# Graph attention on one core: start-up work moved between engines, and the context of blocks 1 to 3 divided by ScalarE in operations of one head

## What is computed

```python
h  = maximum(layernorm(x), 0)                   # sources
hs = layer_norm(h, ln1)                         # masked by nodemask
ht = layer_norm(h_target, ln1)
q = (ht @ Wq + bq) / sqrt(32);  k = hs @ Wk + bk;  v = hs @ Wv + bv
logits = where(adj != 0, q k^T, -1e30)          # [8, 2048, 2048]
ctx = softmax(logits) @ v                       # [2048, 256]
ht = layer_norm(ht + ctx @ Wo + bo, ln2)
out = x + ht + gelu(ht @ W1) @ W2
```

## Time and profile before

| | us |
|---|---|
| median of 3 runs | 715.5 |
| lowest, highest | 714.21, 716.79 |
| the profiled execution, its own time | 714.83 |
| its span, first to last instruction | 713.0 |
| PE busy | 665.8 (93%) |
| DVE busy | 584.3 (82%) |
| POOL busy | 535.8 (75%) |
| ACT busy | 457.4 (64%) |
| mean granted TensorE clock | 0.986 of full |

### The profile page before, as it was taken

The page is one execution under the profiler, slowest core; times in us unless marked ns, Lnnn a source line. Parts: engine busy times, 40 slices in busy tenths (PEclk is TensorE's granted clock), DMA queues, the critical chain, the costliest instruction groups (busy, mean ns, idle before and its releaser), DMA issues. The chain is left out here.

```text
span 713.0 us, 20226 instructions
## 1 busy us (share of the span) xinstructions
PE 665.8 (93%) x8326; PEld 474.8 (67%) x8326; DVE 584.3 (82%) x961; ACT 457.4 (64%) x816; POOL 535.8 (75%) x508
## 2 busy tenths in 40 slices
PE   4987979999999999999999999999999899989998
PEld 4545657676776667667766776777667567657667
DVE  5987768989999977999999699988986988674651
ACT  4644547676776646787766586777655787767550
POOL 3647849889999966799999678999976787552430
PEclk9998989999999999999999999999999999999999
DMA  8721630203000010130010111103000000000001
GB/s 292 263 57 38 208 108 3 90 32 109 28 3 32 2 60 31 61 105 2 2 32 2 60 61 55 38 2 121 2 1 2 2 2 2 2 1 31 16 23 51
DMA packets 20795, 36.20 MB, mean 51 GB/s; under 512 B 2752, under 2 KB 13280, under 8 KB 20704
## 3 DMA queue, kind: packets, MB, share of 16 engines
q1 hardware_dynamic: 20704, 34.92, 15.8%
HBM read 26.49 MB, written 2.10 MB: 40 GB/s over the span
## 5 line engine op out<-in xcount | busy, mean ns | idle before, releaser
L1351 POOL TENSOR_TENSOR prob_lo<-prob 128x512 f16<-128x512 f32 x382 | 436.2, 1166 | 80.8 <-ACT prob L859 80.1
L859 ACT ACTIVATE prob<-score 128x512 f32<-128x512 f32 x512 | 305.1, 597 | 173.4 <-PE score L451 166.2
L451 PE MATMUL early<-kT,qT 96*128 96x512 f16 x512 | 193.9, 384 | 18.7 <-DVE half_max L1140 17.9
L451 PE MATMUL score<-nidentb,mask_nat 128*128 128x128 bf16 x2048 | 200.0, 221 | 3.6 <-ACT qT L876 1.9
L451 PEld LDWEIGHTS ctx<-v_sb,prob 128*128 128x128 bf16 x2048 | 159.8, 98 | 59.8 <-ACT raw L881 10.4
L451 PE MATMUL score<-qT,kT 97*128 97x512 f16 x512 | 197.1, 385 | 0.0
L451 PE MATMUL ctx<-v_sb,prob 128*128 128x65 f16 x2048 | 192.6, 193 | 2.5 <-POOL prob_lo L1351 1.7
L1140 DVE CUSTOM_DVE_ANT_0 early<-early,mask_nat,half_max 128x1024 f32<-128x1024 f32 x128 | 163.0, 1285 | 34.6 <-PE early L451 33.1
L451 PE MATMUL ctx<-v_sb,prob_lo 128*128 128x65 f16 x2048 | 191.4, 193 | 0.0
L1140 DVE CUSTOM_DVE_ANT_0 early<-early,mask_nat 128x1024 f32<-128x1024 f32 x128 | 156.8, 1228 | 25.7 <-PE early L451 24.3
L451 PEld LDWEIGHTS ctx<-v_sb,prob_lo 128*128 128x128 f16 x2048 | 143.7, 97 | 50.3 <-issue 5.1
(11 more groups left out here) (164 smaller groups left out, 615.5 us busy)
## 6 DMA issues: line engine op xcount, KB each, us to landing
adj_in<-in_adj SPq DMA_DIRECT2D x26, 512.0 KB, 3.8
qT<-q_stage SPq DMA_DIRECT2D x48, 64.0 KB, 2.0
kT<-mask_nat SPq DMA_DIRECT2D x48, 64.0 KB, 2.0
raw<-in_x SPq DMA_DIRECT2D x4, 512.0 KB, 5.4
tgt<-in_L_gnn_h_target SPq DMA_DIRECT2D x4, 512.0 KB, 11.8
prob<-in_adj SPq DMA_DIRECT2D x4, 512.0 KB, 10.3
nT<-in_L_gnn_W SPq DMA_DIRECT2D x2, 1024.0 KB, 7.3
mask_nat<-in_x SPq DMA_DIRECT2D x1, 2048.0 KB, 8.5
```

The source lines that it names most:

```text
L451: return nc.tensor.matmul(dst, w, m, start=start, stop=stop, **more)
L859: nc.scalar.activation(prob[:, n % SLOTS, :], score[n % 2][:, :], ACT.Exp).then_inc(exp_done, 1)
L1351: nc.gpsimd.tensor_tensor(prob_lo[:, n % SLOTS, :], prob[:, n % SLOTS, :], prob_hi(n % SLOTS), ALU.subtract).then_inc(lo_sem["pool"], 1)
```

## The change

Ten edits, in five groups.

1. **Start-up, masks of block 0.** Tiles 4 to 7 are made by POOL (`make_mask` in the POOL program, after its memsets) and not by DVE, and counted on a semaphore of their own, `mask_pool`. DVE makes tiles 0 and 1 ahead of `low_parts(3)` and 2 and 3 behind it.
2. **Start-up, feature sum.** POOL's six folds and DVE's reduction go. ACT makes the sum of each half of the features in one operation of 128x2048 with an accumulating output, one ahead of `high_parts(4)` and one behind it.
3. **Start-up, order on PE and SP.** The value products 3 to 7 follow the early products 1 to 5 one by one. SP issues the first two adjacency loads of block 1, then the third and fourth group of placements, and only then waits for the values and loads W1 and W2.
4. **Tables.** The first mask of a next block is made in unit 1 at j = 0 (was unit 0, j = 6), the second at (2, 3) (was (2, 4)). `CT_AT` goes from (2, 6), (2, 11) to (2, 3), (2, 7); the first `WO_AT` from (2, 13) to (2, 11). The last context sum goes from (2, 1) to (1, 11).
5. **The division.** For blocks 0 to 2 (made during blocks 1 to 3) ACT divides, two heads a step: two operations of 128x32 with the reciprocal as a per-partition scale, in four steps for each of the four tiles, beginning at (0, 7), (1, 1), (1, 7) and (1, 12). DVE keeps the division of block 3 and the reciprocals.

```diff
-CT_AT = {(2, 6): 0, (2, 11): 1}
-WO_AT = {(2, 13): 0, (3, 1): 1}
+CT_AT = {(2, 3): 0, (2, 7): 1}
+WO_AT = {(2, 11): 0, (3, 1): 1}
-MASK_DVE = [(0, 6), (2, 4), (2, 6), (3, 2), (3, 7), (4, 3), (4, 7), (5, 3)]
-LOAD_AT = [0, 0, 0, 2, 2, 3, 4, 4]
+MASK_DVE = [(1, 0), (2, 3), (2, 6), (3, 2), (3, 7), (4, 3), (4, 7), (5, 3)]
+LOAD_AT = [0, 0, 1, 2, 2, 3, 4, 4]
-SUM_AT = [(0, 3), (0, 11), (1, 5), (2, 1)]
-NORM_AT = [(0, 5), (1, 1), (1, 5), (2, 2)]
+SUM_AT = [(0, 3), (0, 11), (1, 5), (1, 11)]
+NORM_AT = [(0, 7), (1, 1), (1, 7), (1, 12)]
+NORM_STEPS = H // 2
...
 # SP
                 for c in (2, 3):
                     place_k(c, range(1, 2))
-
-                sp.wait_ge(v_ready, NT // 2)
-                sp.wait_ge(feat_done, 1)
-                for i, (dst, w) in enumerate(((w1, W1), (w2, W2))):
-                    sp.dma_start(dst, w.rearrange("(c p) n -> p c n", p=P)).then_inc(w_in[i], 16)
+                for i in range(2):
+                    load_adj(1, i)
                 for g in range(2, TT):
                     place_q(0, range(g, g + 1))
                     for c in range(NTB):
                         place_k(c, range(g, g + 1))
+                sp.wait_ge(v_ready, NT // 2)
+                sp.wait_ge(feat_done, DC)
+                for i, (dst, w) in enumerate(((w1, W1), (w2, W2))):
+                    sp.dma_start(dst, w.rearrange("(c p) n -> p c n", p=P)).then_inc(w_in[i], 16)
...
 # PE
                 project(4)
-                for e in range(1, TT):
+                for e in range(1, RAMP + 2):
                     for i in range(2):
                         early_scores(e, i)
-                    values(e + 2)
-                values(6)
-                values(7)
-                for e in range(TT, RAMP + 2):
-                    for i in range(2):
-                        early_scores(e, i)
+                    if e + 2 < NT // 2:
+                        values(e + 2)
...
 # ACT
+                def feature_sum(c):
+                    act.wait_ge(nT_masked, DC * NTB)
+                    nc.scalar.activation(unread[:, c, :, :], nT[:, :, c, :], ACT.Copy, accum_out=feat_all[:, c:c + 1]).then_inc(feat_done, 1)
+                def context_norm(k, t, part):
+                    if t == 0 and part == 0:
+                        act.wait_ge(den_done, k + 1)
+                        for g in range(TT):
+                            act.wait_ge(q_placed[g], PLACE * (k + 2))
+                    if part == 0:
+                        act.wait_ge(csum_done, TT * k + t + 1)
+                    for h in (2 * part, 2 * part + 1):
+                        last = nc.scalar.activation(cnorm[:, t, h * HD:(h + 1) * HD], raw_of(k)[:, t, h, 0:HD], ACT.Copy,
+                                                    scale=rden[:, t * H + h:t * H + h + 1])
+                    if part == NORM_STEPS - 1:
+                        last.then_inc(cn_done, 1)
...
                 high_values(2)
+                feature_sum(0)
                 high_parts(4)
+                feature_sum(1)
...
 # ACT, each step, behind the exponential and the other jobs of the step
                         if k > 0:
+                            for part in range(NORM_STEPS):
+                                if (r, s - part) in NORM_AT:
+                                    context_norm(k - 1, NORM_AT.index((r, s - part)), part)
...
 # DVE
-                for i in range(TT):
+                for i in range(2):
                     make_mask(0, i)
                 low_parts(3)
+                for i in range(2, TT):
+                    make_mask(0, i)
+                maxima(0)
                 low_values(2)
-                maxima(0)
-                make_mask(0, 4)
+                maxima(1)
                 low_parts(4)
-                for e in range(1, TT):
+                for e in range(2, RAMP + 1):
                     maxima(e)
-                    make_mask(0, e + 4)
-                for e in range(TT, RAMP + 1):
-                    maxima(e)
-                dve.wait_ge(folded, 6)
-                nc.vector.tensor_reduce(feat_all[:, :], fold[:, 0, :, 0:TB // 8], AX, ALU.add).then_inc(feat_done, 1)
...
-                            if (r, j) in NORM_AT:
-                                context_norm(k - 1, NORM_AT.index((r, j)))
...
 # POOL
+                def make_mask(i):
+                    pool.wait_ge(adj_here[i], 16)
+                    nc.gpsimd.tensor_scalar(mask_half(0, i), adj_home(0, i), 0.0, BIG, ALU.is_equal, ALU.mult).then_inc(mask_pool, 1)
...
-                fold_features(0)
+                for i in range(TT, PAIRS):
+                    make_mask(i)
                 for i in range(V_DVE, NT // 2):
                     low_values(i)
-                    fold_features(i - V_DVE + 1)
```

More of the change, by code:

```diff
@@ L151, in masks_dve @@
 def masks_dve(k, i):
-    return PAIRS * k + i + 1
+    return min(i + 1, TT) if k == 0 else PAIRS * k - TT + i + 1
 def gnn_kernel(nc, x, adj, nodemask, h_target, ln1_scale, ln1_bias, Wq, bq, Wk, bk, Wv, bv, Wo, bo,
@@ L275, in gnn_kernel @@
         v_ready, v_hi, v_lo, v_out, v_lo_pool = sem("v_ready"), sem("v_hi"), sem("v_lo"), sem("v_out"), sem("v_lo_pool")
-        mask_dve = sem("mask_dve")
+        mask_dve, mask_pool = sem("mask_dve"), sem("mask_pool")
         early_ready, max_done = sem("early_ready"), sem("max_done")
@@ L330, in mask_ready @@
         def mask_ready(eng, k, h):
-            eng.wait_ge(mask_dve, masks_dve(k, h * TT + TT - 1))
+            if k == 0 and h == 1:
+                eng.wait_ge(mask_pool, TT)
+            else:
+                eng.wait_ge(mask_dve, masks_dve(k, h * TT + TT - 1))
         def masks_free(eng, k):
@@ L428, in _ @@
                         for i in range(PAIRS):
-                            if LOAD_AT[i] == r:
+                            if LOAD_AT[i] == r and u + i > 1:
                                 load_adj(k + 1, i)
@@ L591, in mean_values @@
                 def mean_values():
-                    pe.wait_ge(feat_done, 1)
+                    pe.wait_ge(feat_done, DC)
                     value_read(pe, 4)
@@ L856, in exponential @@
                     elif n == 0:
-                        act.wait_ge(mask_dve, PAIRS)
+                        act.wait_ge(mask_dve, TT)
+                        act.wait_ge(mask_pool, TT)
                     nc.scalar.activation(prob[:, n % SLOTS, :], score[n % 2][:, :], ACT.Exp).then_inc(exp_done, 1)
```

17 lines of the change are left out of this document (3 added, 14 removed).

## The result

The changed kernel takes 699.53 us, the median of four runs (699.08 to 699.65), where the kernel before took 715.12 beside it (714.21 to 716.79). The ratio is 0.9778, with a 95% interval of 0.9759 to 0.9798. The forecast was 697.8 with 694 to 701 as its own range. The four runs of the kernel before lay high: over the 43 runs of it beside the experiments the median is 713.2, and in the group of experiment 9 the same two kernels give 0.9809 [0.9785, 0.9834], a gain of 13.5 us and not 15.6. The profiled execution took 699.08 us and its span is 697.3, so 15.7 us are gone from the span of 713.0, where the sum had 17.3.

What follows compares the result with a forecast made beforehand. PE, busy 93% of the span, was taken as the bound, so only its waits and half clock could be won. Terms 4.5 + 6.6 + 4.1 - 2.5 + 2.5 + 2.1 = 17.3 us off 714.83 gave 697.5; forecast 697.8, range 694 to 701.

Steps and rivals of the forecast that it cites:

- Start-up: Before the main loop: PE projects the last keys without a stop, negation at 63.1 instead of 67.56; gain 4.5 us.
- POOL's masks: Start-up: four int32 masks on POOL at 2.3 to 2.8 us each, ending at 51.2 to 53.2, before their first reader.
- The rival of the 4 us masks: Start-up gives a third: POOL's masks take 4 us each or half clock hits the values; 3 us less, 701; chance 0.15.
- Half clock: Start-up: same loss taken as before at 68 to 74 us; without it 2.3 us more would be won.
- Unit 1 of block 0: DVE's wait for adjacency and two half-clock steps go, as the load precedes 30 placements; gain 4.96 + 2 x 0.82 = 6.6 us.
- Unit 1 of blocks 1 to 3: One gap ahead of an early product in each goes with the divisions taken from DVE; gain 1.73 + 1.72 + 0.64 = 4.1 us.
- DVE swallows 1.5: Unit 1 of blocks 1 to 3: DVE absorbs 1.5 us of extra work, so the remaining reciprocals and mask, 1.35, cost nothing.
- What ACT pays: Division on ACT: six waits of 0.25 beside `row_out` and three of 0.34 behind `context_out`; loss 2.5 us.
- Unit 2: Blocks 1 to 3: excess of 8.2 us falls to 5.7 without division (2, 2), its wait and clock dip; gain 2.5 us.
- The wait at the shift row: Unit 2, step 8: PE waits for ACT to copy out the bank of turning (2, 7); 0.3 becomes 1.2 us.
- POOL's waits: Unit 2 of blocks 1 and 2: POOL nearly full, 16.96 of 17.24 us; 0.9 of waits taken.
- Unit 3: Blocks 1 to 3: first `rows_out` leaves step (2, 15), 0.39 three times, and `out_row` wait goes, 0.3 three times; gain 2.1 us.

Runs made afterwards that it cites:

- experiment 9: The changed kernel once more with no edit, as the level for its group: 699.35 us, ratio 0.9809 to the kernel before.
- experiment 6: Changed kernel with block 0's mask tiles 4 and 5 given back to DVE, only 6 and 7 on POOL: 695.89 us, ratio 0.9765 to the kernel before.
- experiment 1: Changed kernel with the division of blocks 0 to 2 back on DVE, at (0, 5), (1, 1), (1, 5), (1, 7): 699.6 us, ratio 0.9821 to the kernel before.
- experiment 3: Changed kernel's start-up, load and mask-place edits alone; division on DVE at old places, old turning and Wo tables: 702.86 us, ratio 0.9861 to the kernel before.
- experiment 4: Changed kernel with each ACT division operation made twice for three of the four tiles: 708.42 us, ratio 0.9937 to the kernel before.
- experiment 5: Changed kernel with the second turning of the context at (2, 6) instead of (2, 7): 698.94 us, ratio 0.9792 to the kernel before.
- experiment 7: Changed kernel with ACT's divisions and the context sums moved so divisions fall clear of ACT's other jobs: 697.19 us, ratio 0.977 to the kernel before.
- experiment 8: Changed kernel with no next-block mask in unit 1, masks made from (2, 3) to (6, 3), loads following: 696.26 us, ratio 0.9757 to the kernel before.
- experiment 10: Changed kernel with the last targets' statistics moved from unit 2 of block 1 to unit 7 of block 0: 699.33 us, ratio 0.9809 to the kernel before.
- experiment 2: Kernel before with only the division moved to ACT and the fourth context sum at (1, 11): 708.5 us, ratio 0.9929 to the kernel before.
- the mended one: Changed kernel with the edits of experiments 5, 6, 8 and 10: 694.26 us with division on DVE, 695.7 on ACT with experiment 7's edit too.
- experiment 11: Changed kernel with the edits of experiments 5, 6, 7, 8 and 10 together, division on ACT: 695.7 us, ratio 0.9758 to the kernel before.

## Why the prediction was right, and where it was off

The time, the sign and the range were right; the sum was 1.6 us too large against the two traces, and some 4 against the median of all runs of the kernel before (713.2 and 699.5, 13.7 us). The forecast was counted from an execution of 714.83 us at a granted clock of 0.986, which is one of the longer ones of that kernel, and so were the four runs measured beside the result: that the level came out so close is partly luck.

**Start-up, 4.5 forecast, 5.45 found.** The order of events was the one foretold. Two of its terms were wrong, and neither counted. POOL's masks took 3.6 to 3.9 us each, above the 2.8 that was my upper bound from POOL operations of 256 columns, so POOL became the last to arrive; but DVE's masks 2 and 3 took 1.28 us for both, where I had counted with the 3.42 of before. The rival of the 4 us masks had the right price, but its 3 us of loss against the forecast did not come: the first maximum behind the masks was 0.7 us later than forecast, and when experiment 6 took half of them away the negation moved by 0.7 us. Part of the 5.45 is scatter: with the same start-up edits the first score stands between 63.95 and 64.92 in the traces of the changed kernel and of experiments 1, 3, 4, 5, 7, 8, 9 and 10, and the end of unit 0 between 83.06 and 83.83, but at 82.21 in experiment 5, where half clock lasted half as long. Half clock stayed, as taken; the four short runs of experiment 6 put 2.9 us on it, where the prediction had 2.3.

**Unit 1 of block 0, 6.6 forecast, 5.09 found.** The load went ahead of the placements (two issues at 55.50) and DVE no longer waits for it; the 4.96 and the half clock are gone as forecast. The step that failed is the one not taken: the mask, moved to (1, 0), was given no price there. It takes 1.40 us, and a low part behind it 1.52 beside POOL; one early product is late by 1.45.

**Unit 1 of blocks 1 to 3, 4.1 forecast before ACT's waits, 2.9 found** (2.07 and three waits of 0.26). This is the same error in another dress. I had read from two units that "DVE swallows 1.5", as if slack could be taken from anywhere in the unit, and so held the mask and the reciprocals free. It can't: what is free depends on how far ahead of its early product the operation stands. Experiment 8 shows that the gaps of 0.8 in blocks 1 and 2 were the mask alone. In block 3, where there is no mask, no gap is left but ACT's 0.26.

**What ACT pays, 2.5 forecast, 2.8 found.** Six waits of 0.26 and three of 0.41, at the steps named, with operations of 0.317 us and pairs of 0.42. This was the best step of the prediction. Experiment 7 moved the divisions and all nine waits went.

**Unit 2, 0.75 net forecast, 0.93 found**, once the moved turning is set right. The wait at the shift row was forecast at 1.2 and is 1.21; experiment 5 moved the turning and won 0.9 of it. POOL's waits were taken as 0.9 in each of blocks 1 and 2, and what is left at that step is 0.1 to 0.2; the long DVE operation cost 1.45 in block 1 in their place. That the sum agrees is partly luck.

**Unit 3, 2.1 forecast, 2.16 found.** Experiments 1 to 3 show that it hangs on `CT_AT` and `WO_AT` alone.

**What the prediction didn't ask**, and should have, is what the division itself is worth beside the other edits. My sum books its gain under unit 1 and its cost under ACT, as 4.1 and 2.5. Experiment 1 measures the whole: 699.6 against 699.53, nothing, with the long DVE operation's 1.45 us in one of the two traces. The Trainium skill ("ScalarE: Activation LUTs", Rules for kernel authors) would leave such a multiplication on VectorE. By that rule the move should not have been made; the runs show it neutral in the changed kernel and, by medians of 694.26 and 695.7 whose intervals overlap, no gain in the mended one.

## What to carry to other kernels

Price each moved operation at the place where it lands, by how far ahead of its reader it stands; slack read as a mean over a stage does not cover a single late product. Where several engines are nearly full in the same stretch, a wait that is taken from one can come back on another or in another unit (experiment 7 in the blocks with masks, experiment 10 in sum). So test edits together before judging one, and again each alone inside the last version: here the single gains added up to 7.8 us, and all together gave 3.7 (experiment 11). Look at the granted clock of every run before reading a median: in experiment 6 it carried 2.9 of the 3.6 us. And ask of each moved transfer what stood behind it in its queue: here that, with the work moved about in the start-up and the mask moved to (1, 0), gave 10.3 of the 13.6 us that experiment 1 won.

## What the runs showed of the hardware

- **A DVE operation held until behind a row of POOL's.** A DVE `TENSOR_TENSOR` of 128x512 with both inputs in SBUF took 4.45 to 4.55 us in four traces at the same place (the changed kernel, experiments 5, 6 and 9) and 5.62 in experiment 11, each time while POOL made seven of its own back to back in 7.02 us and until 0.5 us behind their end. In experiments 7 and 10, with seven in a row at the same place, the two engines shared instead: DVE took 1.55 and 1.39 us, and POOL's seven 7.92 and 8.35. Rows of twelve and fourteen stand in every trace, and none of them held a DVE low part for more than 1.6 us. So the row alone doesn't do it; what does stays open. It costs 1.45 us where one early product hangs on it, and more where half clock follows.
- **Int32 to bf16 masks on POOL.** 128x1024 with two scalar operations took 3.6 to 3.9 us, where DVE took 0.68 to 0.69 at the least, mostly 0.9 to 1.7 beside POOL, and 2.3 and 2.8 at the longest in the start-up. The estimate scaled from POOL's float32 operations of the earlier trace rows was 2.3 to 2.8.
- **A sum over 2048 columns on ACT** with an accumulated output took 1.90 us and 0.19 more to read the accumulator.
- **Scatter that goes with the granted clock.** The kernel before spreads over 709.3 to 716.8 us over all its runs, the changed one over 698.98 to 699.76. Beside the experiments, the runs of the kernel before at 709.3 to 709.8 us had a mean granted clock of 0.992 or 0.993, those above 714.9 one of 0.985 or 0.986; the changed kernel had 0.995 in all eight. DVE's wait for adjacency was 3.6 us in one trace of the old order, with 7 us at half clock behind it, and 1.6 in that of experiment 2, with 3.4; that the spread comes from this wait is argued from these two traces only.
